# Paged attention in a four-layer chain: value pages gathered by indirect transfers from POOL instead of sixteen page transfers from SP

## The chip, the cores and the metric

The kernel runs on one NeuronCore of one Trainium2 chip. Its engines are TensorE (PE, its weight loads PEld), VectorE (DVE), ScalarE (ACT), GpSimd (POOL) and SyncE (SP, which only issues transfers). The metric is the device time of one execution in microseconds (us). The kernel before takes 2593.76 us (median of 3 runs, 2591.18 to 2595.24).

## What is computed

A batch of 64 sequences of 32 tokens with 512 features goes through four residual layers: an adapter matmul, two layers with low-rank adapters, and a paged attention. The change touches only the attention, which for each sequence computes:

```python
# HQ=32 query heads, HK=8 key/value heads, D=128, 16 pages of 32 keys a sequence
q, k, v = split(x @ W.T); q, k = rope(rmsnorm(q)), rope(rmsnorm(k))
kc = k_cache[block_table].reshape(bsz, 512, HK, D)       # 16 pages named by the table
vc = v_cache[block_table].reshape(bsz, 512, HK, D)
k_all, v_all = concat([kc, k]), concat([vc, v])          # 512 cached keys + 32 own
scores = where(valid, q @ k_all.T * SCALE, -1e30)        # 4 query heads share a key head
x = x + (softmax(scores) @ v_all) @ Wo.T
```

The table is 64 sequences x 16 page numbers out of 64 pages. All is float32; products with keys are made from a high and a low part of each operand.

## The kernel before

The attention stage works sequence by sequence (s = 0 to 63), with two of every input buffer, chosen by p = s % 2. A sequence has eight units of work, one per key head; its four query heads with 32 tokens each fill 128 rows. A loop body of `in_pairs` covers two sequences, 16 units numbered j, u over all sequences.

For a unit u, PE makes the scores of u + 2, then the outputs of u - 4 (probabilities times values), then the transposes of the probabilities of u (`pair` from L1528). DVE masks the scores and takes the maximum (L1403), ACT exponentiates (L1337) and copies the transposed probabilities out of PSUM (`copy_pt`, L1344). Between these, ACT and DVE split the raw keys and queries of a coming sequence into their parts, in six pieces: four of four key pages each, the queries (piece 3) and the sequence's own keys (piece 5). `HI_AT` and `LO_AT` (L1148, L1149) say at which j % 8 ACT and DVE do which. ACT splits pieces 0 and 1 of sequence s + 2 at the last two units of s, and the other pieces, own keys first and queries third, at the first units of s + 1. The semaphore `lo_done` counts the pieces that DVE has finished, and so says when a raw buffer is free.

Transfers have two issuers, and each works through its list in program order:

- SP (L1227 to L1275) reads a sequence's 16 page numbers into registers (`pages_in`) and issues 16 transfers of one key page (128 KB, 128 partitions x 1 KB) and 16 of one value page (128 KB, 32 partitions x 4 KB). The order in the loop is keys of s + 2, values of s + 1, for both parities in turn. Keys wait for `lo_done`; values wait for `pv_done`, which counts PE's finished outputs, until all of sequence s - 2 are out.
- POOL (L1277 to L1330) issues, for each s, the sequence's own values (4 transfers, after the same wait on `pv_done`), the queries and own keys of s + 2 (after `lo_done`), and then the stores of output and inverse sums of s - 2 (after `o_ready`, `inv_ready`).

PE waits for the values of a sequence before the outputs of its first head (L1511, L1512). ACT waits for each piece before it splits it (L1349).

The other stages (three layers before, the output projection after) are not touched.

Of the kernel before, what the change touches and what calls it, by code (L numbers as in the profile page):

```python
# [18 lines left out]
i32 = mybir.dt.int32  # L19
ALU = mybir.AluOpType  # L20
# [3 lines left out]
P = 128  # L24
NSEQ, SEQ, D = 64, 32, 512
# [55 lines left out]
def later(t, n):  # L81

    return not isinstance(t, int) or t >= n
# [1071 lines left out]
NB_P = OG  # L1155
V_ORDER = [c * PPP + m for c in range(NPP // PPP) for m in (0, 2, 1, 3)]

# [5 lines left out]

def attention(nc, pool_sems, k_pages, v_pages, table, lens, key_at, q_t, k_own, v_own, o_t, inv_t):

# [3 lines left out]
    with ExitStack() as ctx:  # L1169
# [10 lines left out]
        lens_sb, lens_f, key_sb = m.sb("lens", [P, NSEQ], i32), m.sb("lens_f", [P, NSEQ]), m.sb("key_at", [P, NKEY])  # L1180
        table_sb = m.sb("table", [1, NSEQ * NPP], i32)
        mask = m.sb("mask", [P, 2, NALL])
# [9 lines left out]

        zeroed, ident_ready, table_loaded = m.sem("zeroed"), m.sem("ident_ready"), m.sem("table_loaded")
        small_loaded, lens_ready, mask_ready = m.sem("small_loaded"), m.sem("lens_ready"), m.sem("mask_ready")
# [3 lines left out]
        v_loaded = m.sems("v_loaded", 2)  # L1198
        hi_done, lo_done = m.sem("hi_done"), m.sem("lo_done")
# [26 lines left out]
        with nc.Block() as block:  # L1226
            @block.sync  # L1227
            def _(sp):
                sp.dma_start(lens_sb[:, :], lens).then_inc(small_loaded, 16)
                sp.dma_start(key_sb[:, :], key_at).then_inc(small_loaded, 16)  # L1230

                def pages_in(s):

                    return nc.values_load_multi_w_load_instructions(
                        table_sb[:, bass.ds(s * NPP, NPP)], engines=[mybir.EngineType.SP], min_val=0,
                        max_val=NPAGE - 1, skip_runtime_bounds_check_because="block tables name pages")[1]
# [12 lines left out]
                def load_v(s, p, pages):  # L1249

                    if later(s, 2):
                        sp.wait_ge(pv_done, HK * (s - 1))
                    for n in V_ORDER:
                        at = n % PPP * PSIZE
                        sp.dma_start(v_sb[at:at + PSIZE, p, n // PPP, :], v_pages[bass.ds(pages[n], 1)])\
                          .then_inc(v_loaded[p], 16)

                sp.dma_start(table_sb[:, :], table).then_inc(table_loaded, 16)
                sp.wait_ge(table_loaded, 16)
                pages = pages_in(0)  # L1260
                load_k(0, 0, pages)
                load_v(0, 0, pages)
                load_k(1, 1, pages_in(1))

                def pair(i, last):

                    if not last:
                        next_pages = pages_in(2 * i + 2)
                        load_k(2 * i + 2, 0, next_pages)
                    load_v(2 * i + 1, 1, pages_in(2 * i + 1))  # L1270
                    if not last:
                        load_k(2 * i + 3, 1, pages_in(2 * i + 3))
                        load_v(2 * i + 2, 0, next_pages)

                in_pairs(sp, NSEQ // 2, pair)  # L1275

            @block.gpsimd  # L1277
            def _(pool):
# [11 lines left out]
                def load_own_v(s, p):  # L1290

                    if later(s, 2):
                        pool.wait_ge(pv_done, HK * (s - 1))
                    rows = v_own[bass.ds(s * SEQ, SEQ), :].rearrange("k (g u d) -> k g u d", g=HK // OG, u=OG)
                    for u in range(OG):
                        pool.dma_start(vo_sb[u * SEQ:(u + 1) * SEQ, p, :, u, :], rows[:, :, u, :])\  # L1296
                            .then_inc(own_v_loaded[p], 16)

                def store(s, p):
# [12 lines left out]
                pool.memset(vo_sb[:, :, :, :, :], 0.0).then_inc(zeroed, 1)  # L1312
                pool.wait_ge(zeroed, 3)

                def pair(i, last):
                    for p in range(2):
                        s = 2 * i + p
                        load_own_v(s, p)
                        if not last:
                            load_q(s + 2, p)  # L1320
                            load_own_k(s + 2, p)
                        if later(s, 2):
                            store(s - 2, p)

                in_pairs(pool, NSEQ // 2, pair)
                for p in range(2):
                    store(NSEQ - 2 + p, p)
                for p in range(2):
# [46 lines left out]
            def _(dve):  # L1375
                dve.wait_ge(small_loaded, 32)
                dve.tensor_copy(lens_f[:, :], lens_sb[:, :]).then_inc(lens_ready, 1)
                dve.wait_ge(lens_ready, 1)
                dve.wait_ge(zeroed, 2)

                def make_mask(s, p):

                    dve.tensor_scalar(mask[:, p, 0:NKEY], key_sb[:, :], lens_f[:, bass.ds(s, 1)], MASKED,
                                      ALU.is_ge, ALU.mult).then_inc(mask_ready, 1)
                    dve.wait_ge(mask_ready, s + 1)

# [87 lines left out]
            def _(pe):  # L1474
# [231 lines left out]
def conditioned_stack(nc, i, out):  # L1706
# [8 lines left out]
    with ExitStack() as ctx:  # L1715
# [6 lines left out]
        qkv(nc, x3, i["w_qkv"], i["lens_tok"], i["inv_freq"], i["step_pos"], i["norm_w"], q_t, k_own, v_own)  # L1722
        attention(nc, pool_sems, i["k_pages"], i["v_pages"], i["table"], i["lens_all"], i["key_at"], q_t,
                  k_own.rearrange("s d c x -> s d (c x)"), v_own, o_t, inv_t)
# [3 lines left out]
def laid_out(a):  # L1728
# [5 lines left out]
    def everywhere(v):  # L1734

        return np.broadcast_to(v.reshape(1, -1), (P, v.size))
# [28 lines left out]
        "v_pages": a["L3_cond_v_cache"].reshape(NPAGE, PSIZE, HK * DH),  # L1765
        "table": a["itok_Bx16_0_63"].reshape(1, -1),
        "lens_all": everywhere(lens),
# [18 lines left out]
```

## Time and profile before

| | |
|---|---|
| median of 3 runs | 2593.76 us |
| the profiled execution itself | 2590.91 us, span 2589.4 us, mean TensorE clock 0.975 |
| busy over the span | PE 94%, PEld 85%, DVE 69%, ACT 61%, POOL 14% |
| attention, from the first transfers to the last store | about 919 to 2190 us |
| DMA over the span | 541 MB, mean 209 GB/s |
| transfers of key pages, value pages | 1024 and 1024, 128 KB each |

The page's busy share is an average over stages. In the attention PE is nearly always busy, so the waits that matter are the few that end at PE. SP does no computing, so its rows are issues of transfers: the time shown for a run of issues is the time from the first to the end of the last. A POOL row of a transfer is the time in which POOL makes its descriptors; the data moves afterwards. Queue q1 in the DMA views carries what SP issues, q0 what POOL issues.

### The profile page before, as it was taken

The numbers are of one execution on the slowest core, as the hardware profiler recorded it, in microseconds if no ns is written. First come the engines' busy times: TensorE is split into PE (matmuls) and PEld (weight loads), VectorE is DVE, ScalarE is ACT, GpSimd is POOL, SyncE is SP. The second block draws the span as 40 slices with busy tenths as digits, with TensorE's granted clock in tenths as the row PEclk, the third lists the DMA queues.
The fourth block names the chain that finished last, engine by engine and source line by source line (L and its number), as shares of the span: only waits on it lengthen the run. The fifth ranks groups of instructions, "written<-read, shape, count | busy, mean of one in ns | idle before, by whom it ended". The sixth has DMA issues, their size and how long they took to land. (4 is left out here: it accounts for less than half of the span.)

```text
span 2589.4 us, 57693 instructions
## 1 busy us (share of the span) xinstructions
PE 2431.1 (94%) x16326; PEld 2206.4 (85%) x16327; DVE 1794.7 (69%) x3684; ACT 1591.8 (61%) x3313; POOL 373.6 (14%) x613
## 2 busy tenths in 40 slices
PE   6699899999999939999999999999999998599999
PEld 5588688888888839999999999999999998488887
DVE  6345346898899848878778777787887775544443
ACT  3122236777787748888878878887887885311111
POOL 1222130000000012222222222222222221000000
PEclk9899899999999969999999999999999999799999
DMA  6422432333332278999999999999999994756664
GB/s 229 144 77 73 140 135 86 110 105 96 100 115 86 82 232 266 283 296 282 285 289 277 279 292 281 285 291 280 285 287 280 283 294 141 290 201 216 217 216 152
DMA packets 388287, 541.08 MB, mean 209 GB/s; under 512 B 61667, under 2 KB 275363, under 8 KB 384356
## 3 DMA queue, kind: packets, MB, share of 16 engines
q1 hardware_dynamic: 352932, 450.10, 56.7%
q0 software_dynamic: 33152, 87.07, 10.1%
q10 hardware_dynamic: 2112, 2.89, 0.4%
q8 instruction: 34, 0.56, 0.1%
q14 instruction: 57, 0.47, 0.1%
HBM read 441.54 MB, written 98.30 MB: 208 GB/s over the span
## 5 line engine op out<-in xcount | busy, mean ns | idle before, releaser
L1518 PE MATMUL att_ps_o<-att_pt,att_v 128*128 128x128 f32 x4096 | 542.7, 276 | 21.0 <-DMA att_v<-in_v_pages 19.1
L1518 PEld LDWEIGHTS att_ps_o<-att_pt,att_v 128*128 128x128 f32 x4096 | 504.8, 192 | 26.1 <-issue 22.4
L1337 ACT ACTIVATE att_prob<-att_prob,att_shift 128x544 f32<-128x544 f32 x512 | 383.8, 750 | 210.0 <-DVE att_shift L1403 196.5
L76 PE MATMUL att_ps_s<-att_k_hi,att_q_hi 128*128 128x272 f32 x1024 | 339.6, 332 | 33.7 <-DVE att_k_lo L1434 22.4
L1403 DVE CUSTOM_DVE_ANT_0 att_prob<-att_ps_s,att_mask 128x544 f32<-128x544 f32 x512 | 366.4, 716 | 0.0
L1434 DVE TENSOR_TENSOR att_k_lo<-att_k_raw,att_k_hi 128x1024 fp32r<-128x1024 f32 (+1 forms) x320 | 338.5, 1058 | 19.1 <-ACT att_k_hi L1352 19.1
L76 PE MATMUL qkv_ps_y<-qkv_w_hi,qkv_xt_hi 128*128 128x512 f32 x768 | 314.8, 410 | 0.0
L1344 ACT ACTIVATE att_pt<-att_ps_pt 128x512 f32<-128x512 f32 x512 | 295.0, 576 | 27.5 <-PE att_ps_pt L1497 25.5
L1352 ACT ACTIVATE att_k_hi<-att_k_raw 128x1024 fp32r<-128x1024 f32 (+1 forms) x320 | 292.8, 915 | 28.4 <-DMA att_k_raw<-in_k_pages 28.4
L1497 PE MATMUL att_ps_pt<-att_ident,att_prob 128*128 128x128 f32 x2048 | 309.1, 274 | 1.0 <-ACT att_pt L1344 1.0
L78 PE MATMUL qkv_ps_y<-qkv_w_hi,qkv_xt_lo 128*128 128x512 f32 x768 | 301.4, 392 | 0.0
L77 PE MATMUL qkv_ps_y<-qkv_w_lo,qkv_xt_hi 128*128 128x512 f32 x768 | 300.8, 392 | 0.0
L78 PE MATMUL att_ps_s<-att_k_hi,att_q_lo 128*128 128x272 f32 x1024 | 298.4, 291 | 0.0
L77 PE MATMUL att_ps_s<-att_k_lo,att_q_hi 128*128 128x272 f32 x1024 | 296.0, 289 | 0.0
L1398 DVE COPY att_p_own<-att_prob 128x32 f32<-128x32 f32 x512 | 90.4, 177 | 260.2 <-PE att_ps_s L78 255.2
L1296 POOL DMA_DIRECT2D att_vo<-v_own x256 | 141.1, 551 | 793.7 <-PE att_ps_o L1521 781.1
L1497 PEld LDWEIGHTS att_ps_pt<-att_ident,att_prob 128*128 128x128 f32 x2048 | 242.7, 142 | 1.2 <-issue 1.2
L1624 ACT ACTIVATE out_o_hi<-out_o 128x2048 fp32r<-128x2048 f32 x32 | 61.4, 1918 | 294.3 <-DVE out_o L1651 294.3
L76 PE MATMUL out_ps_y<-out_w_hi,out_o_hi 128*128 128x512 f32 x512 | 203.3, 397 | 39.9 <-DVE out_w_lo L1644 36.2
L76 PEld LDWEIGHTS att_ps_s<-att_k_hi,att_q_hi 128*128 128x128 f32 x1024 | 195.6, 191 | 35.7 <-issue 22.7
L916 ACT ACTIVATE qkv_normed<-qkv_ps_y,qkv_inv_rms 128x128 f32<-128x128 f32 x640 | 182.5, 368 | 58.0 <-DVE qkv_inv_rms L1026 58.0
L77 PE MATMUL out_ps_y<-out_w_lo,out_o_hi 128*128 128x512 f32 x512 | 202.4, 395 | 0.0
(178 smaller groups left out, 4632.5 us busy)
## 6 DMA issues: line engine op xcount, KB each, us to landing
att_k_raw<-in_k_pages SPq DMA_DIRECT2D x1024, 128.0 KB, 2.8
att_v<-in_v_pages SPq DMA_DIRECT2D x1024, 128.0 KB, 4.3
q_t<-qkv_out_t SPq DMA_DIRECT2D x128, 256.0 KB, 2.3
att_q_raw<-q_t POOLq DMA_DIRECT2D x64, 512.0 KB, 6.4
o_t<-att_o POOLq DMA_DIRECT2D x64, 512.0 KB, 7.2
out_o<-o_t SPq DMA_DIRECT2D x32, 1024.0 KB, 6.4
out_inv<-inv_t SPq DMA_DIRECT2D x32, 1024.0 KB, 7.0
qkv_w_stage<-in_w_qkv SPq DMA_DIRECT2D x12, 1024.0 KB, 5.1
```

The lines of the kernel that those rows point to most:

```text
L76: pe.matmul(out, xh, wh, start=start, stop=False)
L77: pe.matmul(out, xh, wl, start=False, stop=False)
L78: return pe.matmul(out, xl, wh, start=False, stop=stop)
L916: last = act.activation(normed[:, p, h, :], ps_y[:, j % 4, h, :], ACT.Copy, scale=inv_rms[:, p, h:h + 1])
L1296: pool.dma_start(vo_sb[u * SEQ:(u + 1) * SEQ, p, :, u, :], rows[:, :, u, :])\
L1337: act.activation(prob[:, b, :], prob[:, b, :], ACT.Exp, bias=shift[:, b:b + 1], scale=-1.0, accum_out=total[:, j // HK, j % HK:j % HK + 1] ...
L1344: act.activation(pt_sb[:, j % OG, :, :], ps_pt[:, j % 2, :, :], ACT.Copy).then_inc(pt_ready, 1)
L1352: act.activation(hi, raw, ACT.Copy).then_inc(hi_done, 1)
L1403: dve.tensor_tensor_reduce(out=prob[:, b, :].rearrange("p (a n) -> p a n", a=2), in0=ps_s[:, j % 2, :, 0:HALF], in1=mask[:, j // HK, :].re ...
L1434: dve.tensor_tensor(lo, raw, f32(hi), ALU.subtract).then_inc(lo_done, 1)
L1497: mm = pe.transpose(ps_pt[:, j % 2, c, :], prob[:, j % NB_P, c * P:(c + 1) * P], ident[:, :])
L1518: pe.matmul(out, v_sb[:, p, c, h * DH:(h + 1) * DH], pt_sb[:, j % OG, c, :], start=(c == 0), stop=False)
```

## The change

The 16 value transfers of a sequence leave SP. POOL makes four indirect transfers in their place. Each fills all 128 partitions with rows of 4 KB (one key position of one page each, 512 KB in all), and takes its 128 row numbers from a column in SBUF. DVE makes these row numbers once at the stage's start for all sequences (page number x 32 + position within the page), from the table, which is now loaded to all 128 partitions (512 KB instead of 4 KB). POOL copies the four columns of the coming sequence to a fixed place (`rows_now`) ahead of its gathers, between the first and the second transfer of the own values.

POOL's list is also shifted: at its step s it handles the own values and the gathers of s + 1 and the stores of s - 1, where it handled own values of s and stores of s - 2. The queries and own keys of s + 2 keep their place in step s. Semaphores are merged where one was freed for another; SP's first key pages now wait for all four small loads.

```diff
@@ attention, tiles
-        table_sb = m.sb("table", [1, NSEQ * NPP], i32)
+        table_sb, step_sb = m.sb("table", [P, NSEQ * NPP], i32), m.sb("step", [P, 1])
+        row_sb, rows_now = m.sb("row", [P, NSEQ * NPP // PPP], i32), m.sb("rows_now", [P, 2, NPP // PPP], i32)
...
@@ SP
-                def load_v(s, p, pages):
-
-                    if later(s, 2):
-                        sp.wait_ge(pv_done, HK * (s - 1))
-                    for n in V_ORDER:
-                        at = n % PPP * PSIZE
-                        sp.dma_start(v_sb[at:at + PSIZE, p, n // PPP, :], v_pages[bass.ds(pages[n], 1)])\
-                          .then_inc(v_loaded[p], 16)
-
-                sp.dma_start(table_sb[:, :], table).then_inc(table_loaded, 16)
-                sp.wait_ge(table_loaded, 16)
-                pages = pages_in(0)
-                load_k(0, 0, pages)
-                load_v(0, 0, pages)
+                sp.dma_start(table_sb[:, :], table).then_inc(small_loaded, 16)
+                sp.wait_ge(small_loaded, 64)
+                load_k(0, 0, pages_in(0))
                 load_k(1, 1, pages_in(1))
 
                 def pair(i, last):
 
                     if not last:
-                        next_pages = pages_in(2 * i + 2)
-                        load_k(2 * i + 2, 0, next_pages)
-                    load_v(2 * i + 1, 1, pages_in(2 * i + 1))
-                    if not last:
-                        load_k(2 * i + 3, 1, pages_in(2 * i + 3))
-                        load_v(2 * i + 2, 0, next_pages)
+                        for p in range(2):
+                            load_k(2 * i + 2 + p, p, pages_in(2 * i + 2 + p))
@@ POOL
                     for u in range(OG):
+                        if u == 1:
+                            pool.tensor_copy(rows_now[:, p, :], row_sb[:, bass.ds(s * (NPP // PPP), NPP // PPP)])\
+                                .then_inc(rows_copied, 1)
+                            pool.wait_ge(rows_copied, s + 1)
                         pool.dma_start(vo_sb[u * SEQ:(u + 1) * SEQ, p, :, u, :], rows[:, :, u, :])\
                             .then_inc(own_v_loaded[p], 16)
+
+                def load_v(s, p):
+
+                    for c in range(NPP // PPP):
+                        pool.indirect_dma_start(
+                            v_sb[:, p, c, :], None, v_pages.rearrange("n k x -> (n k) x"),
+                            bass.IndirectOffsetOnAxis(ap=rows_now[:, p, c:c + 1], axis=0)).then_inc(v_loaded[p], 16)
...
                 pool.wait_ge(zeroed, 3)
+                pool.wait_ge(rows_ready, PPP + 2)
+                load_own_v(0, 0)
+                load_v(0, 0)
 
                 def pair(i, last):
+
                     for p in range(2):
                         s = 2 * i + p
-                        load_own_v(s, p)
+                        if not (last and p):
+                            load_own_v(s + 1, 1 - p)
+                            load_v(s + 1, 1 - p)
                         if not last:
                             load_q(s + 2, p)
                             load_own_k(s + 2, p)
-                        if later(s, 2):
-                            store(s - 2, p)
+                        if later(s, 1):
+                            store(s - 1, 1 - p)
 
                 in_pairs(pool, NSEQ // 2, pair)
-                for p in range(2):
-                    store(NSEQ - 2 + p, p)
+                store(NSEQ - 1, 1)
@@ DVE, once at the start
+                row_f = prob[:, 0, 0:NSEQ * NPP // PPP]
+                for m_ in range(PPP):
+                    at = slice(m_ * PSIZE, (m_ + 1) * PSIZE)
+                    dve.tensor_copy(row_f[at, :], table_sb[at, :].rearrange("p (n m) -> p n m", m=PPP)[:, :, m_])\
+                       .then_inc(rows_ready, 1)
+                dve.wait_ge(rows_ready, PPP)
+                dve.tensor_scalar(row_f, row_f, float(PSIZE), step_sb[:, 0:1], ALU.mult, ALU.add).then_inc(rows_ready, 1)
+                dve.wait_ge(rows_ready, PPP + 1)
+                dve.tensor_copy(row_sb[:, :], row_f).then_inc(rows_ready, 1)
@@ PE, outputs
-                        pe.wait_ge(v_loaded[p], 16 * NPP * (i + 1))
+                        pe.wait_ge(v_loaded[p], 16 * (NPP // PPP) * (i + 1))
```

POOL, one step of the loop, before. `att_vo` are own values, `att_q_raw` queries, `att_k_raw` from `k_own` own keys, `o_t` and `inv_t` the stores.

```order
L1296 ISA [waits att_pv_done]
L1296 DMA att_vo<-v_own 32x2x128
...
L1282 ISA [waits att_lo_done]
L1282 DMA att_q_raw<-q_t 128x1024
L1287 REGISTER_ALU
L1288 ISA [waits att_lo_done]
L1288 DMA att_k_raw<-k_own 128x256
L1300 REGISTER_ALU
L1301 ISA [waits att_o_ready]
L1301 DMA o_t<-att_o 128x1024
```

The same step of POOL after the change. `att_v` from `in_v_pages` are the gathers.

```order
L1286 ISA [waits att_pv_done]
L1286 DMA att_vo<-v_own 32x2x128
L1283 ISA
L1283 COPY att_rows_now<-att_row 128x4
...
L1286 ISA [waits att_rows_copied]
L1286 DMA att_vo<-v_own 32x2x128
...
L1292 DMA att_v<-in_v_pages,att_rows_now 128x1024 x4
L1267 ISA
L1268 ISA [waits att_lo_done]
L1268 DMA att_q_raw<-q_t 128x1024
L1273 REGISTER_ALU
L1274 ISA [waits att_lo_done]
L1274 DMA att_k_raw<-k_own 128x256
```

The gathers stand between the wait on `pv_done` and the queries and own keys. The wait on `pv_done` at this place is for the outputs of s - 1 in the changed kernel, where it was for those of s - 2 in the same step s; so queries and own keys of s + 2 are issued eight units later than before.

SP in the loop, before: the end of a sequence's key pages, the page numbers, the value pages.

```order
L1246 DMA att_k_raw<-in_k_pages 128x256
L1234 ISA
L1234 TENSOR_LOAD att_table
L1252 REGISTER_ALU
L1255 ISA [waits att_pv_done]
L1255 DMA att_v<-in_v_pages 32x1024
```

The same place of SP after the change: the next sequence's key pages follow at once.

```order
L1247 DMA att_k_raw<-in_k_pages 128x256
L1235 ISA
L1235 TENSOR_LOAD att_table
L1244 ISA
L1247 ISA [waits att_lo_done]
```

## Rows read from the trace of the kernel before

**Rows 1.** Busy time by stretch: attention's steady part, and one sequence of it

```profile
core 0: us, PE busy (x) PEld busy (x) DVE busy (x) ACT busy (x) POOL busy (x), PEclk, DMA share, GB/s
981.30:2157.10 1175.80, 1154.84 (x9943) 1148.37 (x9941) 930.72 (x2197) 953.26 (x1829) 266.81 (x487) 1.00 0.93 284
1018.87:1037.65 18.78, 18.78 (x166) 18.76 (x165) 15.27 (x37) 15.51 (x31) 4.40 (x9) 1.00 0.89 277
```

**Rows 2.** Who waited for whom, 981.3 to 2157.1: us in total, times, longest

```profile
PEld att_ps_o L1518 <- issue: 22.4, 18, 3.8
PE att_ps_o L1518 <- DMA att_v<-in_v_pages: 19.1, 16, 3.6
...
POOL o_t L1301 <- issue: 4.5, 4, 3.9
...
POOL att_q_raw L1282 <- issue: 2.9, 1, 2.9
```

**Rows 3.** Timeline of SP: start us, us, what, times

```profile
1536.05 8.44 SPq L1246 DMA_DIRECT2D att_k_raw<-in_k_pages  x16
1545.87 8.20 SPq L1255 DMA_DIRECT2D att_v<-in_v_pages  x16
1555.44 8.49 SPq L1246 DMA_DIRECT2D att_k_raw<-in_k_pages  x16
```

**Rows 4.** Timeline of POOL: start us, us, what, idle before and its releaser

```profile
981.31 2.39 POOL L1296 DMA_DIRECT2D att_vo<-v_own  x4 [16.72 <-PE att_ps_o L1521]
...
1018.87 2.41 POOL L1296 DMA_DIRECT2D att_vo<-v_own  x4 [12.62 <-PE att_ps_o L1521]
1021.45 0.56 POOL L1282 DMA_DIRECT2D att_q_raw<-q_t  x1 [0.18 <-DVE att_k_lo L1434]
1022.15 0.55 POOL L1288 DMA_DIRECT2D att_k_raw<-k_own  x1
...
1539.13 2.42 POOL L1296 DMA_DIRECT2D att_vo<-v_own  x4 [10.84 <-PE att_ps_o L1521]
...
2157.08 2.19 POOL L1296 DMA_DIRECT2D att_vo<-v_own  x4 [12.62 <-PE att_ps_o L1521]
```

**Rows 5.** Transfers of own values (first row) and own keys: all durations, ns; landing

```profile
L1296 POOL DMA_DIRECT2D att_vo<-v_own x256: 533/554/613, 924.5 to 2158.7; - x128
...
L1288 POOL DMA_DIRECT2D att_k_raw<-k_own x64: 536/553/570, 920.1 to 2122.3; - x64
...
DMA to landing us min/median/max: 4.5/6.2/7.9
```

**Rows 6.** POOL's longest single operation of the stage, ns min/median/max

```profile
L1312 POOL MEMSET att_vo<- x1: 1799/1799/1799, 922.4 to 922.4; 128x2048 f32 x1
```

**Rows 7.** Timeline around the splitting of pieces, all engines

```profile
1027.10 1.22 DVE L1434 TENSOR_TENSOR att_k_lo<-att_k_raw,att_k_hi 128x1024 fp32r<-128x1024 f32 x1
...
1030.82 0.40 ACT L1352 ACTIVATE att_k_hi<-att_k_raw 128x256 fp32r<-128x256 f32 x1
...
1031.13 0.57 ACT L1344 ACTIVATE att_pt<-att_ps_pt 128x512 f32<-128x512 f32 x1
...
1034.41 0.60 PE L1497 MATMUL att_ps_pt<-att_ident,att_prob 128*128 128x128 f32 x4
```

**Rows 8.** DMA queues, 1544.6 to 1546.1: packets, MB, share of 16 engines

```profile
q0 software_dynamic: 114, 0.40, 70.4%
q1 hardware_dynamic: 153, 0.14, 28.7%
```

**Rows 9.** The same, 1550.6 to 1556.1, value pages alone

```profile
q1 hardware_dynamic: 531, 1.45, 102.0%
```

**Rows 10.** Timeline of the stage's start

```profile
923.74 8.16 SPq L1246 DMA_DIRECT2D att_k_raw<-in_k_pages  x16
932.01 8.21 SPq L1255 DMA_DIRECT2D att_v<-in_v_pages  x16
...
948.65 1.06 ACT L1352 ACTIVATE att_k_hi<-att_k_raw 128x1024 fp32r<-128x1024 f32 x1 [12.22 <-DMA att_k_raw<-in_k_pages]
```

More of the change, by code:

```diff
@@ L1155, with attention @@
 NB_P = OG
-V_ORDER = [c * PPP + m for c in range(NPP // PPP) for m in (0, 2, 1, 3)]
 def pages_of(c):
     return (NPP, 1) if c == PIECE_OWN else ((c if c < PIECE_Q else c - 1) * PPP, PPP)
-def attention(nc, pool_sems, k_pages, v_pages, table, lens, key_at, q_t, k_own, v_own, o_t, inv_t):
+def attention(nc, pool_sems, k_pages, v_pages, table, step, lens, key_at, q_t, k_own, v_own, o_t, inv_t):
     with ExitStack() as ctx:
@@ L1191, in attention @@
         ps_o = m.ps("ps_o", [P, 2, OG, P])
-        zeroed, ident_ready, table_loaded = m.sem("zeroed"), m.sem("ident_ready"), m.sem("table_loaded")
-        small_loaded, lens_ready, mask_ready = m.sem("small_loaded"), m.sem("lens_ready"), m.sem("mask_ready")
+        zeroed, ident_ready = m.sem("zeroed"), m.sem("ident_ready")
+        small_loaded, lens_and_masks = m.sem("small_loaded"), m.sem("lens_and_masks")
         q_loaded, own_k_loaded, own_v_loaded, o_stored, inv_stored = pool_sems
@@ L1230, in _ @@
                 sp.dma_start(key_sb[:, :], key_at).then_inc(small_loaded, 16)
+                sp.dma_start(step_sb[:, :], step).then_inc(small_loaded, 16)
                 def pages_in(s):
                     return nc.values_load_multi_w_load_instructions(
-                        table_sb[:, bass.ds(s * NPP, NPP)], engines=[mybir.EngineType.SP], min_val=0,
+                        table_sb[0:1, bass.ds(s * NPP, NPP)], engines=[mybir.EngineType.SP], min_val=0,
                         max_val=NPAGE - 1, skip_runtime_bounds_check_because="block tables name pages")[1]
@@ L1375, in _ @@
             def _(dve):
-                dve.wait_ge(small_loaded, 32)
-                dve.tensor_copy(lens_f[:, :], lens_sb[:, :]).then_inc(lens_ready, 1)
-                dve.wait_ge(lens_ready, 1)
+                dve.wait_ge(small_loaded, 64)
+                dve.tensor_copy(lens_f[:, :], lens_sb[:, :]).then_inc(lens_and_masks, 1)
+                dve.wait_ge(lens_and_masks, 1)
                 dve.wait_ge(zeroed, 2)
+                row_f = prob[:, 0, 0:NSEQ * NPP // PPP]
[7 more added lines that the diff above has]
+                dve.tensor_copy(row_sb[:, :], row_f).then_inc(rows_ready, 1)
                 def make_mask(s, p):
                     dve.tensor_scalar(mask[:, p, 0:NKEY], key_sb[:, :], lens_f[:, bass.ds(s, 1)], MASKED,
-                                      ALU.is_ge, ALU.mult).then_inc(mask_ready, 1)
-                    dve.wait_ge(mask_ready, s + 1)
+                                      ALU.is_ge, ALU.mult).then_inc(lens_and_masks, 1)
+                    dve.wait_ge(lens_and_masks, s + 2)
                 def wait_for_scores(s, u, j):
@@ L1722, in conditioned_stack @@
         qkv(nc, x3, i["w_qkv"], i["lens_tok"], i["inv_freq"], i["step_pos"], i["norm_w"], q_t, k_own, v_own)
-        attention(nc, pool_sems, i["k_pages"], i["v_pages"], i["table"], i["lens_all"], i["key_at"], q_t,
+        attention(nc, pool_sems, i["k_pages"], i["v_pages"], i["table"], i["step_pos"], i["lens_all"], i["key_at"], q_t,
                   k_own.rearrange("s d c x -> s d (c x)"), v_own, o_t, inv_t)
@@ L1765, in laid_out @@
         "v_pages": a["L3_cond_v_cache"].reshape(NPAGE, PSIZE, HK * DH),
-        "table": a["itok_Bx16_0_63"].reshape(1, -1),
+        "table": everywhere(a["itok_Bx16_0_63"]),
         "lens_all": everywhere(lens),
```

2 lines of the change are left out of this document (1 added, 1 removed).

## Prediction

> **What bounds the kernel now.** I read the busy time by stretch first. In attention's steady part PE is busy for 1154.8 of 1175.8 us, and the DMA engines for 93% of it [rows 1]. Both are near full, so the next question is what ends PE's few waits. The view of waits says: the arrival of value pages, 19.1 us in 16 waits, and 22.4 us of "issue" at PE's weight loads of the same line, the same gaps seen by the other queue [rows 2]. No other engine's wait reaches PE.
>
> The timeline of POOL gives the pace. Its transfers of own values start when PE has finished a sequence's outputs; call that moment T. The first T inside the loop is 981.31, the last 2157.08, 61 sequences later [rows 4]: 1175.8 / 61 = 19.27 us a sequence. A sequence in which no value was late takes 18.78 us [rows 1]. So late values cost 61 x 0.49 = 30 us, and that is the most that steady attention can give back without faster PE work.
>
> Why are they late? SP. Its rows are a closed chain: keys from 1536.05 for 8.44 us, values from 1545.87 for 8.20, keys again from 1555.44 [rows 3]. One round is 19.39 us, of which 16.64 are issuing (about 0.52 us a transfer) and the rest reading page numbers and waiting. The buffer for those values was free at T = 1539.13 [rows 4], and SP came to it 6.7 us later. SP's list is longer than PE's 18.78 us.
>
> **What goes.** 16 value issues, 8.2 us, and one reading of page numbers leave SP in every round. It is left with about 10 us for 18.78. Values are then issued by POOL straight after T, with PE needing them a little over one sequence later (8 units of outputs). So PE's waits for values should end: minus 30 us, if nothing else is late.
>
> **What comes late next.** POOL's list. The rows of the order show that queries and own keys of s + 2 now stand behind four gathers and behind the wait for the outputs of s - 1: eight units later than before. Before, own keys were issued 3.28 us after T [rows 4] and read more than a sequence later. Now ACT reads them in the same sequence: its own-key split, at 1030.82, is 11.95 us after T = 1018.87 [rows 4, 7]. Behind that split on ACT stand the copy of transposed probabilities (ends 1031.70) and then the exponentials; the copy has to end before PE's transposes two units on, 1034.41 [rows 7]. That gives 2.7 us of cover. With L for the landing of own keys after T, PE is not touched up to L = 14.65, and beyond it a sequence takes L + 0.88 (split and copy) + 3.24 (from 1034.41 to the next T, 1037.65) = L + 4.12 us.
>
> L has two parts.
>
> By issue: own values 2.41 [rows 4] and 0.4 for the copy of row numbers and its wait (an estimate; it is a tiny copy), then 4X for the gathers, then 0.87 as before between own values' end and own keys' issue: own keys are issued at T + 3.7 + 4X. They land 4.5 (least) to 6.2 us (median) later [rows 5]; I take 5.35. No gather is in this trace, so X is the unknown. From below: the direct form, which also makes descriptors for 128 rows, takes 0.55 us [rows 5]. From above: 1.80 us, POOL's longest operation in the stage [rows 6], though nothing excludes more. A gather must read 128 numbers as well as write 128 descriptors, so I take twice the direct form, 1.1 us. Then L = 3.7 + 4.4 + 5.35 = 13.5.
>
> By bytes: ahead of and with the own keys, POOL's queue carries 2.10 MB of values, 0.52 of queries and 0.13 of own keys. POOL's queue moved 0.40 MB in 1.5 us with keys beside it, 267 GB/s, on 70.4% of the engines: 379 GB/s if alone [rows 8]. I take the flow to start at T + 5.2, that is 1.3 us after the first gather's descriptors (an estimate; in rows 8, at T + 5.5, the queries' transfer issued at T + 2.6 is in full flow). Up to T + 7.4 a piece of keys goes beside it (0.59 MB moved), up to T + 10.7 it is alone (1.25 MB). Then the next piece of keys comes, freed by DVE at 1028.32, T + 9.45 [rows 7]; the last 0.91 MB at 267 GB/s take 3.4 us. With 0.4 for the last completion L = 14.5.
>
> The larger counts: 14.5, just under 14.65. So a sequence takes PE's 18.78 us, with no margin. To this I add 0.2: POOL paused for nothing the profile shows in 5 places for up to 3.9 us [rows 2], which was covered and now is not, and ACT has hardly any idle time in the units after the split to catch up. Forecast 19.0 us a sequence.
>
> One thing helps that the sum needs: values fetched by SP go to 32 partitions each and ran at 1.45 MB in 5.5 us, 263 GB/s with every engine busy [rows 9]; transfers over 128 partitions reach the 379 of rows 8. If gathers behave like these, values cost 5.5 us of all engines in place of 8.0, and the 93% falls to about 81% (0.93 x 19.27 - 2.5, over 19.0).
>
> **The start.** SP's 8.21 us of first value issues stood before the keys of sequence 1, for whose first piece ACT waited 12.22 us, to 948.65 [rows 10]. They go. Against it: SP waits for a 512 KB table (1 to 2 us), DVE's six small operations come before its first split but in its idle time, and POOL now puts 4.2 MB of values of sequences 0 and 1 in front: at 267 GB/s they flow for 16 us, in which the keys beside them get 0.14 MB in 1.5 us, 93 GB/s [rows 8], so the 1.05 MB that ACT waits for need 11 us. Nearly all is given back. I take -1, between -8 (no competition) and +6.
>
> **Sum.** 61 x (19.0 - 19.27) = -17, start -1: the profiled execution of 2590.9 goes to 2573. The median of the runs is 2.9 above the profiled one, so 2576 us.
>
> The Trainium skill speaks against the change (DMA: Bandwidth & Descriptors, "Issuing engines are not separate DMA queues"): all issuers share the same 16 engines, and another issuer only saves the sequencer's time, which it calls usually small beside the transfer. Here 16 issues take 8.20 us and their data about 8, so it is not small. By that rule alone nothing would change, which is rival B.
>
> **Rival A, own keys late, slower than before.** The point where it decides is L = 15.15 (where L + 4.12 = 19.27), X = 1.5 us by issue. At X = 1.8, L = 3.7 + 7.2 + 5.35 = 16.2, the sequence 20.4, +1.1 x 61 = +67, 2660 us. The same comes of a flow of 320 in place of 379 GB/s alone and a start 1 us later. For it: the margin of 0.15 us, the unknown X, and own keys at the end of a long queue. Against: the direct form's durations, 533 to 613 ns [rows 5], show no trouble on POOL, and ACT would be the only one to wait. A variant: each gather also waits for one of DVE's 1.22 us subtractions [rows 7], X = 2.3, L = 18.2, a sequence 22.4, about 2780 us. The skill states such a lock (SBUF: State Buffer, "Who interferes with whom"): a DVE instruction with two SBUF inputs contends with a GpSimd instruction that reads SBUF. The direct transfers read no SBUF operand, so their even durations do not rule it out.
>
> **Rival B, the DMA engines bound.** At 93% share [rows 1] a sequence's 5.4 MB may simply need the time. If the gathers flow no better than rows 9, the saved issue time is lost in the queue and the sequence stays near 19.2: 2588 to 2599 us. Against: in the undisturbed sequence the share was 89% at 18.78 us [rows 1].
>
> **Rival C, all hidden.** X near 0.8 and full flow: 18.78 a sequence and the start's -8: 2590.9 - 30 - 8 + 2.9 = 2556 us.
>
> **Chances.** Forecast with rival C, faster, 0.47; B 0.13; A 0.40, of which the variant 0.08. I call changes below 0.2% (5 us) no change, which is what a measurement of this kernel can tell. The range, 2555 to 2665, runs from C to the plain form of A; the forecast's own range is 2556 to 2587.
>
> **What would show it.** Right: no wait of PE for `att_v`; SP's runs of keys broken by waits for DVE; successive own-value starts on POOL 18.8 to 19.2 us apart; a gather of 1.0 to 1.3 us; own keys landing 14 to 15 us after T; a DMA share below 90%. Wrong: ACT waiting for `att_k_raw` from `k_own` in every sequence (rival A), a gather above 1.5 us, or PE still waiting for `att_v` (rival B).

## The result, and the profile after

The changed kernel takes 2741.84 us (median of 4 runs, 2736.34 to 2745.28) against 2594.5 for the kernel before in the same comparison (2591.18 to 2601.05). The ratio is 1.0571, 95% interval 1.0551 to 1.0592. That is 5.7% slower; the forecast was 2576 us in a range of 2555 to 2665. Own keys are late (rival A), and by more than the prediction priced that rival (2660 us).

The steady part of attention, by stretch, then one sequence from T to the next T (it answers to [rows 1]):

```profile
core 0: us, PE busy (x) PEld busy (x) DVE busy (x) ACT busy (x) POOL busy (x), PEclk, DMA share, GB/s
981.30:2294.50 1313.20, 1182.68 (x9960) 1158.61 (x9959) 949.17 (x2199) 936.25 (x1834) 571.62 (x793) 0.99 0.76 253
1504.70:1526.20 21.50, 19.21 (x163) 18.79 (x163) 15.63 (x37) 15.40 (x31) 9.47 (x14) 1.00 0.78 256
```

PE does the same matmuls in a longer time, at nearly the full granted clock (0.99; 1.00 in the one sequence), and the DMA engines are less busy than before (0.76 against 0.93). PE's idle time has grown from 21 to 131 us. So neither PE nor the DMA engines' total is the limit: something is waited for. From T of sequence 2 to T of sequence 63 (61 sequences) the mean pace is 21.52 us, against 19.27 before: 61 x 2.25 = 137 of the 154 us by which the two profiled spans differ (2743.7 and 2589.4). Another 6.4 lie ahead of the attention's first transfer, 3.6 in its start, 6.6 between the last T and the first transfer of the output stage; the first and the last of these three were not followed up.

Who waited for whom in that part (us in total, times, longest), against [rows 2]:

```profile
ACT att_k_hi L1355 <- DMA att_k_raw<-k_own: 242.9, 60, 6.8
DVE att_k_lo L1448 <- ACT att_k_hi L1355: 203.8, 60, 6.1
...
PEld att_ps_pt L1511 <- issue: 95.5, 60, 4.3
PE att_ps_pt L1511 <- ACT att_pt L1347: 85.8, 60, 4.2
POOL att_v L1292 <- issue: 80.7, 244, 2.0
PEld att_ps_s L1517 <- DVE att_shift L1417: 57.7, 55, 1.1
PE att_ps_s L1517 <- DVE att_shift L1417: 44.7, 55, 0.8
POOL att_vo L1286 <- POOL att_rows_now L1283: 43.2, 61, 0.7
```

PE's wait for `att_v` is gone, as forecast. In its place ACT waits for own keys in 60 of the sequences, and PE waits for ACT. One such case in the timeline of ACT and PE; T is 1504.74:

```profile
1521.86 0.42 ACT L1355 ACTIVATE att_k_hi<-att_k_raw 128x256 fp32r<-128x256 f32 x1 [4.00 <-DMA att_k_raw<-k_own]
1522.18 0.58 ACT L1347 ACTIVATE att_pt<-att_ps_pt 128x512 f32<-128x512 f32 x1
...
1522.91 0.63 PE L1511 MATMUL att_ps_pt<-att_ident,att_prob 128*128 128x128 f32 x4 [1.39 <-ACT att_pt L1347]
...
1526.65 0.33 PE L1517 MATMUL att_ps_s<-att_ident,att_p_own 128*128 128x128 f32 x1 [0.80 <-DVE att_shift L1417]
```

The own keys arrive at T + 17.1. Behind their split stands the copy of the transposes on ACT, and PE's next transposes need it. The row of the next T, 1526.19, is 4.33 us after the split's start. POOL's list in that sequence (answers to [rows 4]):

```profile
1504.74 0.58 POOL L1286 DMA_DIRECT2D att_vo<-v_own  x1 [9.56 <-PE att_ps_o L1535]
1505.32 1.17 POOL L1283 COPY att_rows_now<-att_row 128x4 int32 x1
1507.20 1.75 POOL L1286 DMA_DIRECT2D att_vo<-v_own  x3 [0.72 <-POOL att_rows_now L1283]
1509.26 1.02 POOL L1292 DMA_INDIRECT att_v<-in_v_pages,att_rows_now  x1 [0.30 <-issue]
...
1513.09 0.93 POOL L1292 DMA_INDIRECT att_v<-in_v_pages,att_rows_now  x1 [0.30 <-issue]
1514.01 0.60 POOL L1268 DMA_DIRECT2D att_q_raw<-q_t  x1
1514.57 0.63 POOL L1274 DMA_DIRECT2D att_k_raw<-k_own  x1
1515.12 0.62 POOL L1298 DMA_DIRECT2D o_t<-att_o  x1
```

POOL gets to the own keys at T + 9.83, where it was T + 3.28. And then they need longer to land than in [rows 5]. The durations of all own-key issues and all gathers (ns, min/median/max), and issue to landing:

```profile
L1274 POOL DMA_DIRECT2D att_k_raw<-k_own x64: 536/621/633, 926.5 to 2293.3; - x64
...
DMA to landing us min/median/max: 6.1/7.1/9.3
...
L1292 POOL DMA_INDIRECT att_v<-in_v_pages,att_rows_now x256: 933/966/1944, 940.7 to 2311.1; - x128
...
DMA to landing us min/median/max: 4.1/5.8/8.6
```

Why, the DMA view shows for 1511.3 to 1521.7 (busy share by slices, bytes, then packets, MB and share by queue):

```profile
DMA  8396899998898899969779899899998999999999
...
DMA packets 1260, 3.51 MB, mean 337 GB/s; under 512 B 148, under 2 KB 488, under 8 KB 1260
## 3 DMA queue, kind: packets, MB, share of 16 engines
q0 software_dynamic: 880, 3.16, 88.7%
q1 hardware_dynamic: 380, 0.35, 9.6%
```

The same for the 3.4 us before, 1507.9 to 1511.3:

```profile
DMA packets 500, 0.49 MB, mean 145 GB/s; under 512 B 88, under 2 KB 445, under 8 KB 500
...
q0 software_dynamic: 103, 0.13, 21.4%
```

So the flow sets in at about T + 6.5. Then for 10.4 us, up to about the moment at which own keys land, POOL's queue alone holds nearly nine tenths of all 16 engines. The keys are the last 0.13 MB of 2.75, and the stores behind them have begun to flow as well (3.16 MB moved). SP's cached keys get 0.35 MB in that time. So the low DMA share is an average of two things: a queue filled to the brim, and a pause around T, until the first gather is issued.

Four sequences, nine apart (T at 1547.0, 1741.8, 1936.6 and 2131.7), are longer than the others: 25.4 to 26.0 us, where the other 57 take 21.2. In each, POOL pauses for 1.95 us between its first and its second gather, for no reason that the profile shows; own keys are issued at T + 11.9 instead of T + 9.8, and PE waits 3.65 to 4.17 us. The granted clock falls to the lower level (0.50, that is 1.2 of 2.4 GHz): in three of them during that wait and for 6.8 us, in the last 1.0 us after it and for 3.4 us. The pause, PE's wait and the stretch at the lower clock, in the first of them:

```profile
1554.54 0.97 POOL L1292 DMA_INDIRECT att_v<-in_v_pages,att_rows_now  x1 [1.95 <-issue]
```

```profile
1567.47 1.09 PE L1511 MATMUL att_ps_pt<-att_ident,att_prob 128*128 128x128 f32 x4 [3.65 <-ACT att_pt L1347]
```

```profile
1566.52:1573.35 6.83, 5.88 (x27) 5.91 (x28) 5.22 (x11) 6.83 (x14) 0.53 (x1) 0.50 0.49 161
```

The four transposes of that row take 1.09 us, against 0.63 at the full clock in the row of 1522.91 above. Together the four long sequences cost 4 x 4.5 = 18 of the 137 us.

### The profile page after: what moved, and what is told of

The parts are those of the page before. It is cut to its first block and busy times, and to the rows that moved or that the text cites. A ratio compares the mean times of both kernels' runs of the same rounds, so it can differ in the third digit from the quotient of the medians.

```text
span 2743.7 us, 55459 instructions
## 1 busy us (share of the span) xinstructions
PE 2460.0 (90%) x16326; PEld 2216.3 (81%) x16327; DVE 1811.8 (66%) x3690; ACT 1572.4 (57%) x3313; POOL 692.3 (25%) x933
## 5 line engine op out<-in xcount | busy, mean ns | idle before, releaser
L1292 POOL DMA_INDIRECT att_v<-in_v_pages,att_rows_now x256 | 251.4, 982 | 84.3 <-issue 84.3
```

Of the source, the lines that this page charges most:

```text
L1292: pool.indirect_dma_start(v_sb[:, p, c, :], None, v_pages.rearrange("n k x -> (n k) x"), bass.IndirectOffsetOnAxis(ap=rows_now[:, p, c:c + ...
```

## The experiments

All kernels below carry one small edit, also the control: in the first layer a wait of PE counts to the tile's number instead of to the adapter's, which is held in a register. "Changed" kernels are to be compared with the control. T, the pace (mean of 61 sequences) and the turn of own keys (medians) come from each run's trace; the times are medians of 4 runs (10 for e2 and e6).

| run | us | ratio to before, 95% | pace | own keys issued, landed after T |
|---|---|---|---|---|
| e0 control | 2715.8 | 1.0439 to 1.0474 | 21.12 | 9.5, 16.3 |
| e1 keys first | 2659.9 | 1.0234 to 1.0268 | 20.19 | a sequence earlier |
| e2 before, shifted | 2593.9 | 0.9987 to 1.0013 | 19.23 | 3.3, 9.5 |
| e3 no row copy | 2686.9 | 1.0330 to 1.0364 | 20.66 | 9.1, 16.1 |
| e4 queries, own keys by SP | 2571.7 | 0.9909 to 0.9946 | 18.78 | by SP |
| e5 plain transfers | 2679.3 | 1.0325 to 1.0363 | 20.44 | 6.9, 15.7 |
| e6 one gather of four | 2590.4 | 0.9991 to 1.0010 | 18.78 | a sequence earlier |
| e7 gathers spread | 2573.2 | 0.9917 to 0.9953 | 18.81 | a sequence earlier |
| e8 keys between | 2572.9 | 0.9900 to 0.9938 | 18.78 | 4.1, in time |
| e9 as e4, table row first | 2576.0 | 0.9908 to 0.9943 | 18.78 | by SP |
| e10 keys first, plain | 2570.3 | 0.9883 to 0.9916 | 18.78 | a sequence earlier |
| e11 keys first, gathers later | 2574.1 | 0.9904 to 0.9947 | 18.80 | a sequence earlier |
| e12 control, PE's code moved | 2717.8 | 1.0455 to 1.0490 | 21.02 | 9.3, 15.9 |
| e13 keys first, code moved | 2662.9 | 1.0238 to 1.0272 | 20.28 | a sequence earlier |
| e14 keys first again | 2661.3 | 1.0228 to 1.0265 | 20.22 | a sequence earlier |
| e15 own keys before queries | 2676.1 | 1.0293 to 1.0327 | 20.47 | 8.4, 14.1 |

**Control (e0).**

> The changed kernel with one line of the first layer altered (TensorE waits for the t+1st weight at tile t, a constant, instead of for the weight that the tile's register names); the other experiments carry the same line. All theories: the same time as the changed kernel, 2742 us within 10, a sequence 21.5 us, own keys landing 16.9 us after T.

It takes 2715.8 us, 26 less than the changed kernel, with the same attention. The pace is 21.12 in place of 21.52, so 24 of the 26 us lie in these 61 sequences. The two traces show what differs, though not why one wait in the first layer changes it. The control's granted clock stays at 1.00 throughout this part. Its four long sequences take 22.8 to 23.5 us, which is 10 of the 24 us less. And the control has a second kind of wait besides the one for own keys ("remote", explained below), which the changed kernel has not: ACT waits for own keys for 109 us between 1000 and 2150 in the control, for 214 in the changed kernel.

**Which part hurts: the list's shift, the copy, or the gathers ahead of the keys? (e2, e3, e1)** e2 is the kernel before with POOL's list shifted and SP still fetching values; e3 leaves the row copy out of the loop, so its gathers fetch the rows of sequences 0 and 1 again and again; e1 swaps two pairs of lines:

```diff
-                            load_own_v(s + 1, 1 - p)
-                            load_v(s + 1, 1 - p)
                         if not last:
                             load_q(s + 2, p)
                             load_own_k(s + 2, p)
+                        if not (last and p):
+                            load_own_v(s + 1, 1 - p)
+                            load_v(s + 1, 1 - p)
```

> The kernel before (values by SP), but POOL's list shifted as in the change: queries and own keys of s+2 only after the wait for the outputs of s-1. Theory (the delay hurts only together with the gathers in front): own keys issued 3.3 us and landed 9.4 us after T, below 14.65, so no cost: 2594 us within 8. Rival (the shift alone costs): ACT waits for k_own, 2620 us or more.

> The changed kernel without POOL's copy of row numbers and its wait for sequences from 2 on (left out: these gather the rows of sequences 0 and 1 again; same bytes). If issuing sets when own keys land: they are issued 1.6 us earlier and land so, a sequence 19.9 us, 2742 - 61 x 1.6 = 2644 us. If the bytes in front of them set it: they land 0 to 0.5 us earlier, 2710 to 2742 us.

> The changed kernel, but POOL issues queries and own keys of s+2 before own values and gathers of s+1, so ahead of the wait for outputs. Theory (late own keys set the pace, through ACT): a sequence falls from 21.5 to 18.8 us, no wait of ACT on k_own, 2742 - 61 x 2.7 - about 5 at the end = 2572 us. Rival (the gathers load the DMA engines or POOL so that the stage is bound by them): the pace stays above 20.5 us, 2680 us or more. Values late in their place: PE waits for att_v.

The shift alone costs nothing: 2593.9, ratio 1.0. Without the row copy the pace is 0.46 us shorter. That is not the copy's price: the first gather now starts at T + 2.7, meets one of DVE's subtractions in most sequences, and takes 2.05 us for 0.97. One such case, from the timelines of POOL and DVE of e3:

```profile
1506.14 2.03 POOL L1292 DMA_INDIRECT att_v<-in_v_pages,att_rows_now  x1 [0.30 <-issue]
```

```profile
1506.05 1.23 DVE L1448 TENSOR_TENSOR att_k_lo<-att_k_raw,att_k_hi 128x1024 fp32r<-128x1024 f32 x1
```

So own keys are issued only 0.4 us earlier than in the control, and land 0.2 us earlier, as expected by bytes. The time lies between the two expectations, as the late updates described below, which the control has, are nearly gone in e3. With keys first ACT's wait for own keys is gone, and 56 us with it, but the pace stays 1.4 us above PE's 18.78. A second loss is left, which no theory had. It reads, in the view of waits (1000 to 2150) of e1:

```profile
DVE att_p_own L1412 <- remote: 154.8, 52, 3.4
...
PE att_ps_s L1517 <- DVE att_shift L1417: 60.0, 51, 1.3
ACT att_pt L1347 <- remote: 58.0, 53, 1.5
```

"Remote" is a releaser that has no record of its own close before the wait's end. The trace's semaphore records show what it is: PE's instructions go on starting in time, but about once a sequence the update after its transposes is recorded 1.5 to 2.6 us after their end (58 times in e1, 59 in the control), and scores' updates up to 1.9 us late, while POOL issues gathers. In the changed kernel none of PE's updates in this part is more than 0.02 us late; in e3 they are fewer and shorter (at most 1.6 us after the transposes).

**Taking own keys off POOL, a plain transfer, fewer gathers, spread gathers (e4 to e7).** In e4 SP issues queries and own keys at their turn among its key pages. e5 is the control with this edit (the values used are not those of the table):

```diff
-                        pool.indirect_dma_start(
-                            v_sb[:, p, c, :], None, v_pages.rearrange("n k x -> (n k) x"),
-                            bass.IndirectOffsetOnAxis(ap=rows_now[:, p, c:c + 1], axis=0)).then_inc(v_loaded[p], 16)
+                        pool.dma_start(v_sb[:, p, c, :], v_pages.rearrange("n k x -> (n k) x")[c * P:(c + 1) * P, :])\
+                            .then_inc(v_loaded[p], 16)
```

e6 and e7 have keys first as e1. In e6 SP fetches 12 value pages and POOL makes one gather; e6 also loads the table's first row alone ahead of the rest, as e9 below. In e7 two gathers stand behind the second own-value transfer and one each behind the third and the fourth, and each of these three waits for one more unit of PE (`pool.wait_ge(pv_done, HK * (s - 1) + u)`).

> The changed kernel with queries and own keys taken from POOL's list: SP issues them at their turn within its key pages. POOL still does the copy, the own values, the four gathers and the stores. Theory (two losses): the late own keys go, the loss of about 1.4 us a sequence that the kernel with keys first still has stays: pace about 20.2 us a sequence, time about 2655 (2635 to 2675). Own keys alone: pace 18.8, time about 2590. Transfer engines as the bound (gathers take bandwidth from keys): pace stays near 21.1, time near 2715.

> The changed kernel with each gather replaced by a plain POOL transfer of the same shape (128 partitions, 4 KB each) from fixed rows of the value pages; the values used are therefore not those the table names. Own keys are issued about 4 x (1.27 - 0.6) = 2.7 us earlier, at T + 6.8, and land at T + 13.6, before they are needed. Theory (the late semaphore updates belong to the indirect form): both losses go, pace 18.8, time 2590 (2580 to 2605). Rival (they belong to any 512 KB of software transfers issued in a row): the second loss stays, pace about 20.2, time about 2655. Rival (bytes): near 2715.

> Three of four value groups by SP again (12 pages), one by a gather; queries and own keys ahead of it on POOL; SP's list as before the change. SP's period is 2 us shorter than before, so the value wait of before (30 us in all) should shrink; the gather costs what one gather costs. Theory (loss in proportion to gathers, 1.4 us for four): pace 18.8 + 0.35 = 19.15, time about 2588 (2575 to 2605). Gathers harmless: pace 18.8, time about 2567. Loss fixed for a block however many gathers (for instance from the copy): pace 20.2, time about 2655.

> Keys first as in the kernel with queries and own keys ahead (2660), but own values and gathers spread: the first pair at T, the second one unit later (with its gather), and so on, so that the four gathers cover three units of PE's work instead of 5 us. Theory (each gather delays what the other engines report during its own time, whatever the spacing): the loss stays, pace about 20.2, time 2650 to 2670. Rival (the loss comes from gathers in a burst, through their 2 MB landing together or POOL's write queue filling): pace 18.8 to 19.4, time 2590 to 2620.

e4 refuted what was expected of it: with the same burst of gathers at the same place after T (the first at T + 3.6, as in e1), both losses are gone, pace 18.78. e7 went the way of the rival. e6 has that pace too, but its first sequences are late (T of sequence 2 at 1000.8, at 984.1 in e8), so the total gains nothing; why its start is slow was not followed up.

e5 shows what sets the landing. Its own keys are issued 2.6 us earlier than the control's, and land only 0.6 us earlier. Own keys of e5, and issue to landing:

```profile
L1274 POOL DMA_DIRECT2D att_k_raw<-k_own x64: 536/543/572, 923.4 to 2225.9; - x64
...
DMA to landing us min/median/max: 5.5/8.7/10.7
```

What POOL saved in issuing, the keys spent in the queue. So here the bytes ahead set the landing, hardly the turn of issue. This also says that the indirect form is not the cause of the first loss: with plain transfers, and with no late update in the trace, the kernel is still 3.4% slower than before.

**One swap in the changed kernel (e8), and three more.** e8 puts queries and own keys between own values and gathers:

```diff
                             load_own_v(s + 1, 1 - p)
-                            load_v(s + 1, 1 - p)
                         if not last:
                             load_q(s + 2, p)
                             load_own_k(s + 2, p)
+                        if not (last and p):
+                            load_v(s + 1, 1 - p)
```

e9 is e4 with the table's first row loaded alone ahead of the other small loads, and only that waited for by SP. e10 is e1 with e5's edit. e11 is e1 with the row copy, three own values and the gathers held back by one unit of PE.

> The changed kernel with one swap: queries and own keys of s + 2 stand between the own values and the gathers of s + 1, so they are issued at about T + 4.5 and have only their own 0.65 MB ahead of them in POOL's queue, not the 2.1 MB of the gathers as well. Theory (own keys land late because they stand behind the gathers, in issue and in bytes): they land at T + 10 to 11, the wait goes, pace 18.8 and time about 2573. If the disturbance of the kernel with keys first (late semaphore updates while gathers are issued) comes back: pace about 20.2, time about 2655. Rival (what hurts is the wait on pv_done ahead of them, 8 units later than before): pace stays near 21, time above 2700.

> The kernel in which SP issues queries and own keys (2571.7), with one more edit at the start: SP loads the 4 KB table row first and waits only for it before its first page numbers, the other 127 rows follow. The first key page was issued 9.0 us after the table, 3.9 us before the change. Theory: the first pieces land 3 to 5 us earlier, time about 2567 (2563 to 2571). Rival: the start is set by the 512 KB table and the row numbers anyway, time unchanged at 2571.

> Keys first (2660) with the four gathers replaced by plain POOL transfers of the same shape from fixed value rows (the values used are not those of the table). The own keys are early here, so what is left is the second loss alone. If the late semaphore updates come from the indirect form: pace 18.8, time about 2573. If they come from 2 MB of software transfers in a burst of issues at this place: pace about 20.2, time 2650 to 2660.

> Keys first (2660) with the row copy, the last three own values and the gathers held back by one more unit of PE (2.35 us), still in one burst. If the second loss depends on where the burst falls against PE, ACT and DVE: it changes, pace nearer 18.8, time 2573 to 2620. If any burst costs it: pace stays at 20.2, time 2650 to 2670. Values then land near T + 16, before their use at T + 18.8, so they add nothing.

e8 hits its 2573: the same gathers, the same copy, the same wait, and 142.8 us less than the control. Its attention (984.13 to 2129.70), own-key split and POOL's list:

```profile
984.13:2129.70 1145.57, 1145.57 (x9946) 1144.22 (x9945) 932.30 (x2197) 950.66 (x1831) 548.88 (x793) 1.00 0.87 291
```

```profile
1510.42 0.58 POOL L1286 DMA_DIRECT2D att_vo<-v_own  x1 [7.38 <-PE att_ps_o L1537]
...
1513.83 0.56 POOL L1268 DMA_DIRECT2D att_q_raw<-q_t  x1 [0.16 <-issue]
1514.52 0.72 POOL L1274 DMA_DIRECT2D att_k_raw<-k_own  x1
1515.55 1.03 POOL L1292 DMA_INDIRECT att_v<-in_v_pages,att_rows_now  x1 [0.30 <-issue]
...
1522.38 0.40 ACT L1357 ACTIVATE att_k_hi<-att_k_raw 128x256 fp32r<-128x256 f32 x1
```

PE has no idle time at all in 61 sequences, and ACT splits the own keys at T + 11.96 without waiting, as in [rows 7]. e9's start edit brought nothing (2576.0). e10 and e11 lose the second loss: plain transfers don't have it, nor do gathers one unit later. e5 and e10 are the pair that sizes the first loss by itself: the same plain transfers, no late updates in either, own keys behind them or a sequence earlier, 2679.3 against 2570.3, 109 us.

**Is the second loss a matter of chance or of where the code lies? And is the first one bytes? (e12 to e15)** e12 and e13 are control and keys first with eight transposes of the identity on PE ahead of the attention; e14 is e1's program once more; e15 is the control with `load_own_k` ahead of `load_q`.

> The control (2715.8, where the changed kernel itself takes 2741.8 with the same attention) with eight extra transposes of the identity on TensorE ahead of the attention's first scores, under 2 us of work once. The changed kernel has eight more PE instructions (register moves) in its first layer than the control; their place in PE's program is the only difference. If where instructions lie decides the second loss: the time moves by 10 us or more, towards 2742. If not: 2714 to 2720.

> Keys first (2659.9) with the same eight extra transposes on TensorE ahead of the attention. If the second loss of that kernel (1.4 us a sequence, with semaphore updates of all engines late while gathers are issued) hangs on where instructions lie in memory: time anywhere from 2573 to 2700, off 2660 by over 10. If it belongs to the order of work: 2657 to 2665.

> Keys first once more, the same program as the one that took 2659.9 (2657.0 to 2664.2). If its second loss is a property of the program: 2655 to 2665. If it hangs on where the program and its tensors were placed when it was loaded: another time, most likely 2573.

> The changed kernel with own keys issued ahead of the queries instead of behind them: 0.57 us earlier in issue, and 0.5 MB less ahead of them in POOL's queue. By bytes (queue moves about 330 GB/s at that time): they land 1.6 us earlier, the pace falls from 21.12 to about 19.5, time about 2620 (the queries, wanted 4.6 us earlier than own keys a sequence on, may then be late themselves: up to 2680). By issue alone: 0.57 us a sequence, time about 2680. Rival (own keys don't set the pace): 2716.

e12 to e14 repeat the times of e0 and e1 within 3.1 us. So the second loss is not the chance of one load of the program, and eight more instructions at this place of PE's code don't move it. The order of the attention's work doesn't settle it alone either: the changed kernel has the control's order and no late update. In e15 own keys land 2.1 us earlier for 1.1 us in issue; the rest goes with the 0.52 MB no longer ahead. ACT's wait for them falls to 25.0 us (109.2 in the control), but "remote" waits of DVE rise to 161.1 (141.9), so the pace stops at 20.47. Both expectations for it, by bytes and by issue, took the pace to follow the landing alone; the second loss was not in them.

## Why the prediction was wrong, point by point

- **What goes: right.** PE no longer waits for values; SP's values were the limit of the kernel before. e8 and e4 show the full worth: 18.78 a sequence, the 30 us that the prediction named as the most there is.
- **Own keys as what is late next: the right place, and the rule for its price held.** "A sequence takes L + 4.12": with the measured L of 16.92 that is 21.04, measured 21.52. What the rule lacks is a second wait of PE, for DVE's maxima, as ACT catches up (the two rows on L1517), and the four sequences of 25.4 to 26.0 us. For POOL's pauses the prediction had added 0.2 us a sequence, rightly in kind: these four sequences cost 0.3 us a sequence in the mean, part of it by the granted clock at its lower level, which the sum had nowhere.
- **L is the step that failed: 13.5 by issue and 14.5 by bytes, against 16.92.** By issue: the copy and its wait took 1.17 + 0.72 = 1.89 us, not 0.4; a gather 0.97 + 0.30 = 1.27 us (median and gap), not 1.1, inside the bounds; together the own keys' issue is at T + 9.8 for 8.1. The landing took 7.1 us, for 5.35: a duration of the kernel before, from a queue that had 0.5 MB ahead of the keys. By bytes: the flow starts at about T + 6.5, not T + 5.2 (the copy again), and the 2.75 MB take 10.4 us, not 9.3, because the stores issued behind them share the engines. These two terms are the whole miss of 2.4 us, and past the cover of 14.65 each 1 us counts in full, 61 times.
- **The margin.** A forecast with 0.15 us of margin should have been priced as about as likely late as not. e5 shows that even transfers issued at the lower bound of X = 0.55 are late: 2679 us. The chance of 0.40 for rival A was too low, and the range's upper end of 2665 rested on the gather's duration alone, with the landing and the copy at fixed values.
- **Rival A's variant: right in kind, rare in this kernel.** A gather that starts while one of DVE's subtractions runs does wait for it. In the changed kernel that is the exception: 228 of the 256 gathers have none beside them, the median stays 0.97, and only 7 start with 0.3 us or more of a subtraction still to run; these take 1.16 to 1.94 us. In e3 64 gathers do, and take 1.31 to 2.08 us (the variant had 2.3). In all of them the gather ends 0.80 to 0.92 us after the subtraction. The copy meets one nearly always: in the trace it takes 0.20 us where no subtraction holds it (6 of 61) and 1.12 to 1.18 in the other 55, and ends 0.04 us after it. The Trainium skill (SBUF: State Buffer, "Who interferes with whom") says that a DVE instruction with two SBUF inputs contends with a GpSimd instruction that reads SBUF; the traces agree, for the copy and for the gather, which reads its row numbers there.
- **Rival B: refuted.** At 18.78 us a sequence e8's engines are busy for 87% (0.93 before at 19.27): 16.3 us of them a sequence, for 17.9. The forecast had 15.4. Issuing elsewhere did pay here.
- **The start: -1 forecast, +3.6 measured.** The first key page was issued 9.0 us after the table (3.9 before), as SP waits for the 512 KB. e9, with one row waited for, issued it 4.7 us after the table's first row (5.6 in e4, its base), but it then landed 8.2 us after its issue (2.0 in e4), and nothing was won.

Still open: what makes PE's semaphore updates late in e0, e1, e12 to e15 and, less, in e3. All of these issue four indirect gathers in one burst, the first at T + 3.6 to T + 4.1 (medians; e3 at T + 2.7), with queries and own keys behind them on POOL. It is absent with plain transfers (e5, e10), with the burst 1.5 us or more later than e1's (e8, e11), spread (e7), with one gather (e6), and with queries and own keys on SP (e4). That list is no rule: the changed kernel's burst starts at T + 4.5 and has no late update, while the control has late updates in its sequences whose first gather comes at T + 4.5 as well. So why the changed kernel lacks them, and has the longer waits for own keys and the lower clock instead, stays open with it.

## What to carry to other kernels

When a transfer is moved to another issuer's queue, write down what stands behind it there and by when each of those is needed, in bytes as well as in turns: with 2 MB put ahead of a small transfer with a deadline the attention took 137 us more than before, and putting the small one first turned 4.6% slower (e0) into 0.8% faster (e8). A landing time read in one queue is no forecast for another: own keys took 6.2 us before, 7.1 in the changed kernel and 8.7 in e5. Where a forecast passes its deadline by less than the error of its terms, price the miss and make the order robust instead.

## What the runs showed of the hardware

- A gather by row numbers, 128 rows of 4 KB, holds POOL for 0.97 us plus a gap of 0.30; the plain transfer of the same shape takes 0.55. The two land alike: medians 5.8 (changed kernel) and 6.15 us (e5). A gather that starts under a subtraction of DVE (1.22 us, two inputs in SBUF) ends 0.80 to 0.92 us after it, so it takes up to 2.08 us (e3).
- POOL's queue, once filled, took 88.7% of the engines over 10.4 us while SP's key pages waited (median 5.3 us from issue to landing over the run, against 2.8 before); the engines are not shared evenly. POOL's queue moved 880 packets there and SP's 380; no run changed the packets' size, so the reason is not shown.
- The granted clock fell from 1.00 to 0.50 during or just after single waits of PE: for 6.8 us at waits of 3.65 to 3.91 us in the changed kernel, for 3.4 us at waits of 4.17 and 1.96 us there and of 3.42 and 3.62 us in the kernel before. In the control it stayed at 1.00 through waits of 2.7 to 3.4 us.
- PE's semaphore updates can come microseconds after the instruction. In e14 PE's transposes end at about 1539.2 and their update is recorded at 1541.79; ACT's copy starts at 1541.82. DVE's row there:

```profile
1541.89 0.18 DVE L1412 COPY att_p_own<-att_prob 128x32 f32<-128x32 f32 x1 [3.01 <-remote]
```
